# Longer runs of gathers and scatters on GpSimd, and eight message slots

## The chip, the cores and the metric
The kernel runs on one core of a Trainium2 chip. The metric is the device time of one execution in microseconds (us), as the median of several runs. TensorE (PE), VectorE (DVE), ScalarE (ACT), GpSimd (POOL) and SyncE (SP) are the core's engines. Each runs its own list of instructions, and they keep in step by semaphores.

## The reference
The kernel computes one layer of a graph network over 50000 nodes with 128 float32 features, and 50000 edges, sorted by receiver (`dst`):

```
w   = MLP(radial_embedding(edge_length))            # 8 -> 64 -> 64 -> 128, silu
ss, vv = (x_scalars @ W_up0)[senders], (x_vectors @ W_up1)[senders]
mid = products of w, ss, vv and the edge's direction  # 64 scalars, 64 vectors
msg = segment_sum(mid, receivers) @ W_out           # back to 128 features
x   = layernorm(x + msg / 16)
```

So each edge gathers the row of its sender from `x`, makes a message of 128 numbers, and adds it to the row of its receiver. Receivers are unevenly spread: many edges end at low node numbers. The second part normalises all 50000 rows.

## The kernel before
**Units.** The edges are dealt into 98 units of four tiles with 128 edges each, from the highest receivers down. The dealing is such that tiles which follow each other closely lie apart in the sorted order; neighbouring pieces of the order stand four tiles apart. A table `scatter_orders`, computed in the kernel, says for each unit how far the copy of `x` must have come and whether its tiles share rows.

**The accumulator.** SyncE copies `x` to the internal tensor `acc`, in 80 pieces of 312.5 KB from the high rows down (`acc_init`). Each unit's messages are added to `acc` by four indirect DMAs of 128 rows, `scatters` (line 470, `acc<-msg,index`). The rows of the senders come by four indirect DMAs, `gathers` (line 444, `sender<-in_x_dram,index`). All 784 are issued by GpSimd.

**The arithmetic of a unit.** TensorE transposes the gathered rows (`turn`, line 531), projects them, runs the two hidden layers and the weights, then sums equal receivers by a matmul with the equality matrix `same` and projects out. ScalarE moves results from PSUM and applies silu. VectorE forms products (`products`), the equality matrix and the count of earlier equal receivers (`equal_receivers`, line 923, one comparison per tile whose two inputs are in SBUF), and the rows to scatter to (`receiver_rows`). ScalarE writes the finished message of unit v to slot v % `RING` of the tile `msg` (`msg_out`, lines 672 and 673). From unit `RING` on it waits until the unit that had the slot has been scattered.

**The dense part.** As `acc` becomes final from the top, SyncE loads chunks of 1664 rows (`total<-acc`, 832 KB, line 343, 30 of them), VectorE takes the statistics (line 986 and following), ScalarE normalises (line 724) and SyncE stores. A table `dense_orders` gives each pair of units its chunk. SyncE waits in pair j for the landing of both units (`landed`) and loads the chunk that stands for pair j + 5; VectorE takes that chunk's first statistics in its pair j + 4, ScalarE normalises it in its pair j + 5. SyncE does all this in order.

**GpSimd's order, which the change touches.** GpSimd's program is written out for all units. It gathers units 0 to 5 first (`LAG` is 6). Then, for each pair of units v, v + 1: read the two entries of the table (line 450), gather units v + 6 and v + 7, scatter units v and v + 1. `sender` has eight slots, so that `gathers(u)` waits until unit u - 8 has been transposed (line 440), and each gather waits for the landing of the gather four tiles ago (line 443). A scatter waits for the needed pieces of `acc_init` (lines 454, 455), for its rows (457) and its message (458), for the landing of the scatter four tiles ago (line 463, three in the first two units), and, where the table says that rows are shared, of the one just before (line 468).

Of the kernel before, what the change touches and what calls it, by code (L numbers as in the profile page):

```python
# [24 lines left out]
P = 128  # L25
# [9 lines left out]
G = 4  # L35
ROWE = G * P
UNITS = -(-E // ROWE)
FULL = E // ROWE
TILES = UNITS * G
PAIRS = UNITS // 2  # L40
LAG = 6
RING = 4
SRING = 8
BATCH = 2
STATS_AFTER = 4
NORM_AFTER = STATS_AFTER + 1
RATE = 3 / 4
# [14 lines left out]
ROUNDS = 3  # L62
SSTEPS = 5 + 3 * ROUNDS
RSQRT_BITS = float(0x5f3759df)
assert UNITS % 2 == 0 and LAG <= SRING and UNITS % BATCH == 0 and (UNITS - 2) % G == 0 and (UNITS - 2) % SRING == 0 and UNITS <= P and FULL == UNITS - 1 and FULL >= 96
assert NORM_AFTER > STATS_AFTER and NORM_AFTER > RING // 2 and (UNITS - 2) % RING == 0 and CHUNKS % 2 == 0 and PIECES % 2 == 0 and N % PIECE == 0 and N - CHUNK - (CHUNKS - 1) * STEP in range(REST + 1)


def bass_gnn(nc, x, src, dst, edge_vec, edge_len, W_up0, W_up1, w0, b0, w1, b1, w2, b2, W_out0, W_out1, out):
# [5 lines left out]
    with ctx:  # L75
        def sb(name, shape, dt=F32):
            return ctx.enter_context(nc.sbuf_tensor(name, shape, dt))
# [85 lines left out]
        sumT = sb("sumT", [P, 2, G, 2, P])  # L163
        msg = sb("msg", [P, RING, G, D])

# [231 lines left out]
        def _(pool):  # L397
# [35 lines left out]
            def here(u, i):  # L433

                return (slot_done[u][i], 16) if u < 2 else (gathered[u % 2][i], 16 * (u // 2))

            def gathers(u):

                if u >= SRING:
                    pool.wait_ge(senderT_ps, u - SRING + 1)  # L440
                for i in range(G):
                    if u >= 1:
                        pool.wait_ge(*here(u - 1, i))
                    pool.indirect_dma_start(sender[:, u % SRING, i, :], None, x,  # L444
                                            bass.IndirectOffsetOnAxis(ap=index[:, u, 0, i:i + 1], axis=0)
                                            ).then_inc(here(u, i)[0], 16)

            def order_of(v):

                return pool.value_load(scatter_orders[0:1, v:v + 1], min_val=2, max_val=2 * PIECES - 1)  # L450

            def scatters(v, order):

                pool.wait_ge(acc_init[0], 16 * (order // 4) + 16)  # L454
                pool.wait_ge(acc_init[1], 16 * ((order + 2) // 4))  # L455
                meets = order % 2
                pool.wait_ge(rows_ready, v + 1)
                pool.wait_ge(msg_ready, v + 1)
                for i in range(G):
                    n = G * v + i  # L460
                    far = 3 if v < 2 else 4
                    if n >= far:
                        pool.wait_ge(*landed(n - far))
                    for of in range(n - far + 1, n) if i == 0 else (n - 1,):
                        if of >= 0:

                            to, count_after = landed(of)
                            pool.wait_ge(to, count_after - 16 + 16 * meets)  # L468
                    pool.sem_inc(pool_passed, 1)  # L469
                    pool.indirect_dma_start(acc, bass.IndirectOffsetOnAxis(ap=index[:, v, 1, i:i + 1], axis=0),  # L470
                                            msg[:, v % RING, i, :], None, compute_op=ALU.add
                                            ).then_inc(slot_done[v % 2][i], 16)
# [3 lines left out]
                gathers(u)  # L476
            pool.wait_ge(spare_rows, 16)
            pool.wait_ge(scatter_tables, 1)
            for v in range(0, UNITS, BATCH):
                orders = [order_of(u) for u in range(v, v + BATCH)]  # L480
                for u in range(v + LAG, min(v + LAG + BATCH, UNITS)):
                    gathers(u)
                for u in range(v, v + BATCH):
                    scatters(u, orders[u - v])


# [131 lines left out]
        def _(act):  # L618
# [46 lines left out]
            def msg_out(v, k):  # L665
                b = k % 2
                act.wait_ge(msg_ps, v + 1)
                slot = bass.ds(v % RING, 1)
                if k >= RING:
                    for i in range(G):  # L670
                        act.wait_ge(slot_done[b][i], 8 * (v - b) - 8 * RING + 32)
                act.copy(msg[:, slot, :, 0:MUL].rearrange("p s i k -> p (s i) k"), ps_msg[:, :, 0:MUL])  # L672
# [405 lines left out]
```

## Time and profile before

| | us |
|---|---|
| median of three runs | 1268.94 (1268.22 to 1271.01) |
| profiled execution | 1267.58 |
| its span, first to last instruction | 1265.8 |
| POOL busy | 1007.1 (80%) |
| PE busy | 860.4 (68%) |
| DVE busy | 695.9 (55%) |
| ACT busy | 535.5 (42%) |

The mean granted TensorE clock was 0.842 of full speed. Busy times count an engine's instructions only; the time that its sequencer needs to issue a DMA is idle time before it, named "issue". The releaser of an idle time is what the semaphores name as last. The HBM moved 123 GB/s over the span.

### The profile page before, as it was taken

To read this page: it belongs to the slowest core of one execution; us is meant where nothing else is said; L and a number is where in the kernel's file an instruction comes from. 1 tells how busy PE (TensorE), PEld (TensorE's weight loads), DVE (VectorE), ACT (ScalarE), POOL (GpSimd) and SP (SyncE) were. 2 spreads that over 40 slices of the span, in tenths; PEclk is the share of its full clock that TensorE was granted. 3 is DMA by queue.
4 is the path that set the end of the run, shared out by engine and by line. 5 is a ranking of instruction groups with operands and counts; after the bars stand their busy time and mean duration, and the time that the engine had idled before them with its cause. 6 is when DMAs were issued, how large, how long until landed. Compare 5 with 4: busy or idle time off the path is not lost.

```text
span 1265.8 us, 25804 instructions
## 1 busy us (share of the span) xinstructions
PE 860.4 (68%) x6206; PEld 817.6 (65%) x6206; DVE 695.9 (55%) x2905; ACT 535.5 (42%) x1416; POOL 1007.1 (80%) x818
## 2 busy tenths in 40 slices
PE   1899775776677667766776677667756775677550
PEld 1799665776577657765776577567756775677550
DVE  6766443575466556565476366446654656446422
ACT  5445322354355245434443435335524533444321
POOL 7778788878877887888778887887888788877885
PEclk9989888888888888888888888878887888788875
DMA  5788784444444443543444443444444354353434
GB/s 161 189 182 193 188 191 71 71 97 93 96 95 98 93 95 46 147 94 41 100 120 69 93 108 87 93 94 97 98 93 95 57 136 94 41 115 84 89 36 86
DMA packets 82645, 130.55 MB, mean 103 GB/s; under 512 B 16168, under 2 KB 66859, under 8 KB 81328
## 3 DMA queue, kind: packets, MB, share of 16 engines
q0 software_dynamic: 68992, 51.43, 31.1%
q1 hardware_dynamic: 12936, 77.36, 17.5%
q10 hardware_dynamic: 680, 1.38, 0.3%
q14 instruction: 28, 0.23, 0.1%
q8 instruction: 9, 0.15, 0.1%
HBM read 78.40 MB, written 77.31 MB: 123 GB/s over the span
## 4 chain that ended last, share of the span: by engine, by line
POOL 44%; issue 27%; DMA 19%; POOLq 4%; SPq 2%; PE 2%; DVE 1%; ACT 0%; DVEq 0%; ACTq 0%
POOL acc L470 30%; POOL sender L444 14%; DMA acc<-msg,index 8%; DMA acc<-in_x_dram 6%; DMA sender<-in_x_dram,index 5%; POOLq L450 2%; POOLq L468 1%; POOLq L469 1%; SPq L307 1%; POOLq L455 0%; PE ps_sum L572 0%; PE ps_wts L559 0%; PE ps_msg L584 0%; PE ps_hid L543 0%; POOLq L454 0%
## 5 line engine op out<-in xcount | busy, mean ns | idle before, releaser
L470 POOL DMA_INDIRECT acc<-msg,index x392 | 616.8, 1573 | 120.8 <-issue 107.5
L444 POOL DMA_INDIRECT sender<-in_x_dram,index x392 | 382.9, 977 | 124.7 <-issue 110.4
L543 PE MATMUL ps_hid<-hid,mlp 128*128 128x256 f32 x196 | 86.3, 532 | 328.3 <-ACT hid L687 328.3
L957 DVE TENSOR_TENSOR wts<-ps_wts,bias 128x512 f32<-128x512 f32 x98 | 67.7, 691 | 423.5 <-PE ps_wts L559 423.5
L543 PEld LDWEIGHTS ps_hid<-hid,mlp 128*128 128x128 f32 x196 | 38.8, 248 | 336.5 <-ACT hid L687 336.5
L572 PEld LDWEIGHTS ps_sum<-same,mid 128*128 128x128 f32 x1568 | 238.1, 224 | 11.5 <-DVE mid L972 0.8
L572 PE MATMUL ps_sum<-same,mid 128*128 128x128 f32 x1568 | 244.8, 308 | 0.7 <-DVE mid L972 0.7
L672 ACT COPY msg<-ps_msg 128x128 f32 (+1 forms) x98 | 26.0, 265 | 426.5 <-DMA acc<-msg,index 381.2
L584 PE MATMUL ps_msg<-outw,sumT 128*128 128x64 f32 x1568 | 185.9, 272 | 0.0
L584 PEld LDWEIGHTS ps_msg<-outw,sumT 128*128 128x128 f32 x1568 | 182.8, 192 | 0.0
L663 ACT COPY sumT<-ps_sum 128x512 f32<-128x512 f32 x196 | 114.6, 584 | 143.0 <-PE ps_sum L572 141.6
L724 ACT ACTIVATE normed<-total,shift,rstd 128x128 f32 x392 | 157.4, 482 | 34.9 <-DVE shift L1022 31.2
L559 PE MATMUL ps_wts<-mlp,hid 128*128 128x128 f32 x784 | 133.5, 327 | 0.6 <-ACT hid L699 0.6
L559 PEld LDWEIGHTS ps_wts<-mlp,hid 128*128 128x128 f32 x784 | 126.9, 245 | 1.3 <-ACT hid L699 1.3
L552 PE MATMUL ps_up<-up,senderT 128*128 128x128 f32 x784 | 115.3, 291 | 6.6 <-DVE mid L964 6.6
L552 PEld LDWEIGHTS ps_up<-up,senderT 128*128 128x128 f32 x784 | 96.5, 194 | 18.6 <-issue 7.0
L986 DVE BATCH_NORM_STATS2 stats<-total 128x6 f32 x392 | 78.8, 278 | 33.8 <-DMA total<-acc 32.9
L950 DVE TENSOR_TENSOR proj<-ps_up,vec_all 128x384 f32<-128x384 f32 x98 | 54.2, 553 | 74.3 <-issue 40.3
L923 DVE CUSTOM_DVE_ANT_0 junk<-same,earlier 128x128 f32<-128x128 f32 x392 | 91.4, 289 | 3.4
L538 PE MATMUL ps_hid<-basisT,mlp 32*128 32x128 f32 x392 | 69.8, 297 | 0.2 <-ACT basisT L679 0.2
L681 ACT COPY senderT<-ps_sT 128x512 f32<-128x512 f32 x98 | 56.5, 577 | 29.3 <-PE ps_sT L531 28.7
L673 ACT COPY msg<-ps_msg 128x384 f32 (+1 forms) x98 | 67.2, 685 | 0.1
(139 smaller groups left out, 1035.2 us busy)
## 6 DMA issues: line engine op xcount, KB each, us to landing
acc<-in_x_dram SPq DMA_DIRECT2D x80, 312.5 KB
total<-acc SPq DMA_DIRECT2D x30, 832.0 KB
out_dram<-normed SPq DMA_DIRECT2D x29, 832.0 KB, 4.2
sender<-in_x_dram,index POOLq DMA_INDIRECT x392, 2.6
acc<-msg,index POOLq DMA_INDIRECT x392, 3.3
out_dram<-normed ACTq DMA_DIRECT2D x1, 832.0 KB, 3.6
vec_raw<-in_edge_attr_dram SPq DMA_DIRECT2D x1, 576.0 KB
acc<-zeros SPq DMA_DIRECT2D x1, 320.0 KB, 4.1
```

Of the source, the lines that this page charges most:

```text
L444: pool.indirect_dma_start(sender[:, u % SRING, i, :], None, x, bass.IndirectOffsetOnAxis(ap=index[:, u, 0, i:i + 1], axis=0)).then_inc(her ...
L470: pool.indirect_dma_start(acc, bass.IndirectOffsetOnAxis(ap=index[:, v, 1, i:i + 1], axis=0), msg[:, v % RING, i, :], None, compute_op=ALU.add
L538: mm = pe.matmul(ps_hid[:, q, :], mlp0[:, q, :], basisT[:, b, :], start=True, stop=True)
L543: pe.matmul(ps_hid[:, 2:4, :], mlp1[:, :], hid0[:, k % 2, :], start=True, stop=True).then_inc(hid1_ps, 1)
L552: mm = pe.matmul(ps_up[:, i, :], senderT[:, b, P * i:P * (i + 1)], up[:, :], start=True, stop=True)
L559: mm = pe.matmul(ps_wts[:, i, :], hid1[:, b, P * (i // 2):P * (i // 2 + 1)], mlp2[:, i % 2, :], start=True, stop=True)
L572: mm = pe.matmul(ps_sum[r][:, i, h, :], mid[:, b, 2 * r + i, P * h:P * (h + 1)], same[:, b, 2 * r + i, :], start=True, stop=True)
L584: mm = pe.matmul(ps_msg[:, i, 2 * MUL * h:2 * MUL * (h + 1)], sumT[:, b, i, h, :], outw[:, h, :], start=True, stop=True)
L663: act.copy(sumT[:, b, 2 * r:2 * r + 2, :, :], ps_sum[r][:, :, :, :]).then_inc(sum_ready[r], 1)
L724: mm = act.activation(normed[:, b, r, :], total[:, quarter, r, :].rearrange("p b d -> p (b d)"), ACT.Identity, scale=rstd[:, b, r:r + 1], ...
L923: mm = dve.tensor_tensor_reduce(junk[:, b, i, :], same[:, b, i, :], earlier[:, :], 1.0, 0.0, ALU.mult, ALU.add, count[:, b, i:i + 1])
L986: mm = dve.bn_stats(stats[:, r, :], total[:, quarter, r, :].rearrange("p b d -> p (b d)"))
```

## The change
The ring of message slots grows from four to eight. GpSimd handles four units in a batch, not two: it reads four table entries, issues the gathers of four units (16 DMAs) and then the scatters of four units (16 DMAs). The first batch keeps two units, since (98 - 2) divides by four. The gathers still run to six units past the end of the batch. ScalarE's program follows the ring: its first `2 * (RING // 2 + 1)` units are written out, now 10 and not 6, and its loop over pairs starts at pair 5; the table has no chunk for the pairs before. Nothing else changes.

```
-RING = 4
+RING = 8
 SRING = 8
-BATCH = 2
+BATCH = 4
...
-            for v in range(0, UNITS, BATCH):
-                orders = [order_of(u) for u in range(v, v + BATCH)]
-                for u in range(v + LAG, min(v + LAG + BATCH, UNITS)):
-                    gathers(u)
-                for u in range(v, v + BATCH):
+            gathered_to = LAG
+            for v, w in [(0, 2)] + [(v, v + BATCH) for v in range(2, UNITS, BATCH)]:
+                orders = [order_of(u) for u in range(v, w)]
+                while gathered_to < min(w + LAG, UNITS):
+                    gathers(gathered_to)
+                    gathered_to += 1
+                for u in range(v, w):
                     scatters(u, orders[u - v])
```

## Rows read from the trace of the kernel before

**Rows 1.** Busy and costliest groups of the page: busy us, mean ns, idle before.
```profile
L470 POOL DMA_INDIRECT acc<-msg,index x392 | 616.8, 1573 | 120.8 <-issue 107.5
L444 POOL DMA_INDIRECT sender<-in_x_dram,index x392 | 382.9, 977 | 124.7 <-issue 110.4
```

**Rows 2.** Waits: engine, line, releaser, total us, times, longest us.
```profile
ACT msg L672 <- DMA acc<-msg,index: 381.2, 45, 10.3
...
DVE stats L986 <- DMA total<-acc: 32.9, 2, 25.8
...
POOL acc L470 <- DMA acc<-msg,index: 11.2, 34, 1.1
...
POOL sender L444 <- PE ps_sT L531: 0.3, 1, 0.3
POOL acc L470 <- DMA acc<-in_x_dram: 0.3, 1, 0.3
POOL acc L470 <- ACT msg L673: 0.3, 1, 0.3
```

**Rows 3.** Timeline of POOL, one round: start, duration, instruction, idle before.
```profile
603.61 1.02 POOL L444 DMA_INDIRECT sender<-in_x_dram,index  x1 [0.30 <-issue]
604.93 0.98 POOL L444 DMA_INDIRECT sender<-in_x_dram,index  x1 [0.30 <-issue]
606.21 0.94 POOL L444 DMA_INDIRECT sender<-in_x_dram,index  x1 [0.30 <-DMA sender<-in_x_dram,index]
607.46 0.94 POOL L444 DMA_INDIRECT sender<-in_x_dram,index  x1 [0.30 <-issue]
...
613.70 1.62 POOL L470 DMA_INDIRECT acc<-msg,index  x1 [0.30 <-issue]
615.63 1.58 POOL L470 DMA_INDIRECT acc<-msg,index  x1 [0.30 <-issue]
617.52 1.57 POOL L470 DMA_INDIRECT acc<-msg,index  x1 [0.30 <-DVE index L937]
619.39 1.55 POOL L470 DMA_INDIRECT acc<-msg,index  x1 [0.30 <-issue]
621.25 1.55 POOL L470 DMA_INDIRECT acc<-msg,index  x1 [0.30 <-issue]
...
628.68 1.02 POOL L444 DMA_INDIRECT sender<-in_x_dram,index  x1 [0.30 <-issue]
```

**Rows 4.** Timeline of POOL, the last run of 32 scatters, first two and last.
```profile
1193.98 1.62 POOL L470 DMA_INDIRECT acc<-msg,index  x1 [0.30 <-issue]
1195.91 1.59 POOL L470 DMA_INDIRECT acc<-msg,index  x1 [0.30 <-issue]
...
1251.86 1.57 POOL L470 DMA_INDIRECT acc<-msg,index  x1 [0.30 <-issue]
```

**Rows 5.** Windows: stretch and length, busy us and count by engine, clock, DMA share, GB/s.
```profile
83.24:1193.98 1110.74, 790.08 (x5729) 752.06 (x5727) 620.16 (x2622) 483.01 (x1283) 895.46 (x705) 0.85 0.48 99
1193.98:1253.41 59.43, 21.00 (x149) 19.89 (x149) 15.84 (x69) 10.46 (x23) 49.98 (x32) 0.69 0.46 65
```

**Rows 6.** Chain of waits around 599 us: POOL's sequencer reads two table entries.
```profile
598.51 0.16 POOLq L450
...
599.26 0.02 POOLq L450
```

**Rows 7.** Timeline of ScalarE: messages of units 2 and 3 written.
```profile
74.67 0.27 ACT L672 COPY msg<-ps_msg 128x128 f32<-128x128 f32 x1 [0.94 <-PE ps_msg L584]
...
82.23 0.27 ACT L672 COPY msg<-ps_msg 128x128 f32<-128x128 f32 x1 [0.94 <-PE ps_msg L584]
```

**Rows 8.** Line 470: landings from 580 us, from 60 to 380, from 1236; a load.
```profile
DMA to landing us min/median/max: 3.2/3.3/3.6
...
DMA to landing us min/median/max: 3.2/3.4/5.6
...
DMA to landing us min/median/max: 3.2/3.3/3.5
...
1240.89 0.36 SPq L343 DMA_DIRECT2D total<-acc  x1
```

**Rows 9.** Timelines of POOL and VectorE around the fourth gather of the next round.
```profile
632.53 1.04 POOL L444 DMA_INDIRECT sender<-in_x_dram,index  x1 [0.30 <-issue]
...
632.46 0.28 DVE L923 CUSTOM_DVE_ANT_0 junk<-same,earlier 128x128 f32<-128x128 f32 x1
```

More of the change, by code:

```diff
@@ L64 @@
 RSQRT_BITS = float(0x5f3759df)
-assert UNITS % 2 == 0 and LAG <= SRING and UNITS % BATCH == 0 and (UNITS - 2) % G == 0 and (UNITS - 2) % SRING == 0 and UNITS <= P and FULL == UNITS - 1 and FULL >= 96
+assert UNITS % 2 == 0 and LAG <= SRING and (UNITS - 2) % BATCH == 0 and (UNITS - 2) % G == 0 and (UNITS - 2) % SRING == 0 and UNITS <= P and FULL == UNITS - 1 and FULL >= 96
 assert NORM_AFTER > STATS_AFTER and NORM_AFTER > RING // 2 and (UNITS - 2) % RING == 0 and CHUNKS % 2 == 0 and PIECES % 2 == 0 and N % PIECE == 0 and N - CHUNK - (CHUNKS - 1) * STEP in range(REST + 1)
```

## The prediction
> **What bounds the kernel now.** I read the busy times first. GpSimd (POOL) is the busiest engine, and two instructions make up nearly all of its 1007.1 us: 392 scatters and 392 gathers, 1573 and 977 ns each [rows 1]. The idle times come next. Before a gather or scatter POOL idles 0.30 us, the same for both kinds, and the profile finds no releaser for most of it (107.5 and 110.4 us in all). A real wait is rare: 11.2 us over 34 scatters for an earlier scatter's landing, one gather for TensorE's transpose, one scatter for a message, 0.3 us each [rows 2]. In the other direction, ScalarE waited 381.2 us in 45 places, up to 10.3 us, to put a message into a slot that a scatter had not yet left. So the arithmetic waits for POOL, never POOL for the arithmetic. From 83.24 to 1193.98 us POOL runs 44 equal rounds of eight scatters and eight gathers, then 32 scatters in a row until 1253.41 us [rows 5]; some 12 us of finishing follow. Whatever shortens POOL's stream by one microsecond ends the kernel one earlier; whatever only speeds up the others gives nothing.
>
> **What a switch costs.** The timeline of POOL through one quiet round is the core of this case; the reader should subtract neighbouring starts [rows 3]. Gathers: 1.32, 1.28, then 1.25 us from start to start. Scatters: 1.93, 1.89, 1.87, then 1.86. The first two gathers after a scatter, and the first three scatters after a gather, are slower than those that follow. Over the settled steps that is (0.07 + 0.03) + (0.07 + 0.03 + 0.01) = 0.21 us a round. The gap stays at 0.30 and the instruction itself is longer (1.02 and 0.98 against 0.94; 1.62 and 1.58 against 1.55), so it is POOL's own work that is slow after a change of kind, not a wait. The last run bears this out: its first two scatters take 1.62 and 1.59 us, and the 32nd 1.57 [rows 4]; the surcharge does not come back with the count of instructions.
>
> **The change part by part.**
> *Longer runs.* Before, a run of gathers stands ahead of each pair of units from v = 2 to v = 90: 45 runs behind the opening 32 gathers. After, one stands ahead of v = 2, 6, ... 90: 23 runs (16 gathers each, the last 8). Scatter runs fall from 46 to 24. So 22 rounds of switching vanish: 22 x 0.21 = 4.6 us. The counts, 392 and 392, stay, and so do the settled steps. The opening and the last 32 scatters are the same in both: units 96 and 97 are gathered ahead of scatter 90 either way.
>
> *Reads of the order table.* Four register loads, not two, now stand ahead of a run of gathers on POOL's sequencer. Two take from 598.51 to about 599.28, 0.8 us [rows 6], while POOL has scatters queued: the gather behind them starts at 603.61 [rows 3]. Four take 1.6 us, and 3.5 us of cover remain: cost 0. Without the cover, 23 x 1.6 less what is hidden today, at most 37 us; with 5.1 us of queued work I take the nil end. A gain isn't possible, as the number of loads is the same.
>
> *Eight message slots.* ScalarE's wait now asks for the scatter of eight units ago. It can run further ahead, which POOL does not notice directly. What is late next: VectorE. Its statistics are paired with units, and a dense chunk is loaded only when the units of four pairs ago have landed; up to now four slots held the arithmetic back more than that, and VectorE waited for a load only twice [rows 2]. I expect that wait to appear in most pairs and to replace part of ScalarE's. Behind it on VectorE stand the next unit's products and rows, so messages stop too. But then six messages are ready, 6 x 4 x 1.86 = 44.6 us of scatters, more than a run of 16 (29.8 us), and the load is a matter of some 5 us. Cost 0.
>
> *Gathers further ahead.* Gather u asks that unit u - 8 has been transposed. For the last of a run that is unit v + 1, transposed before message v - 1 was made, which the preceding scatters already needed. Cost 0. In the first such run (gathers 8 to 11 from 73.0 us on, the scatters of 2 to 5 from about 93 us) messages 2 and 3 were written at 74.67 and 82.23 us already [rows 7], each later one some 7.6 us on, against 7.4 us for a unit's scatters with 18 us of lead.
>
> *Scatter after scatter.* A scatter waits for the landing of the one four before. In a run of eight half of them look back across the gathers; in a run of 16 only a quarter. The distance within a run is 4 x 1.86 = 7.44 us, less the 0.30 that an issue takes: landing may last some 7.1 us. It lasts 3.3 in the middle and at most 5.6 beside the copies of x [rows 8]. Cost 0; the bounds are in the rivals. The pieces of `acc` needed move earlier by less than a round, and POOL's waits for them were one scatter, 0.3 us.
>
> *Irregular lengthening.* The 44 rounds last 1110.74/44 = 25.24 us, the quiet one 628.68 - 603.61 = 25.07 [rows 3, 5]. So 0.17 us a round, 7.5 us in all, is in single instructions that are longer, such as the fourth gather of the next round, 1.04 instead of 0.94 us, while VectorE runs the comparison with two inputs from SBUF [rows 9]. The number of VectorE instructions is unchanged, but the phase between the two engines is not. I take no change; bounds: halved with the rounds, a gain of 22 x 0.17 = 3.7 us; doubled, a loss of 7.5 us.
> The Trainium skill (SBUF — State Buffer, the rules on the shared port pair) says that a VectorE instruction with two SBUF inputs contends with a GpSimd instruction that reads SBUF, and that the later one is blocked until the first ends. The row would allow that reading; the slip of 0.10 us is less than the 0.28 us of the comparison. By the rule a collision depends on phase alone, so it names the cause of the last bound above and not its sign.
>
> **The sum.** The profiled execution took 1267.58 us (span 1265.8 and 1.8 around it); less 4.6 that is 1263.0. The median of the runs is 1268.94, 1.36 higher, so on its scale the forecast is 1264.3.
>
> **The rivals.**
> *More than the switches goes (faster).* If the lengthenings belong to the rounds, since many sit at the same place (third or fourth gather), they halve too: 8.3 us gained, 1260.6. For it: their fixed place. Against: VectorE's work, beside which they occur, is not less.
> *The switch is not saved (no change).* If the slow first instructions come from something else, such as a period in time or in instructions, regrouping moves them only: 1268.9. Against it is the last run of 32, where nothing returns [rows 4].
> *Landings become the bound (slower).* Place: the landing wait inside a run of 16. A dense load of 832 KB goes out when an odd unit has landed. Today that is always the end of a run, so the load falls beside gathers; after the change half of the 30 loads go out in the middle of a run, beside the scatters of the other two units. Price: beside copies of 312.5 KB, landings rose from 3.3 to 5.6, that is 2.3 us; if it grows with size, 2.3 x 832/312.5 = 6.1 and a landing is 9.4 us, 2.3 over the 7.1 allowed. Fifteen loads at 2.3 us are 35 us: 1268.94 - 4.6 + 35 = 1299. It decides once a landing is above about 7.1 + 4.6/15 = 7.4 us. For it: the DMA engines are shared. Against it: in the last run one such load was issued at 1240.89 us amid scatters, and no landing there passed 3.5 us [rows 8].
> The Trainium skill (DMA: Bandwidth & Descriptors, section on queues, rings and completion order) has the rule that speaks against the change: each DMA engine serves its queue rows in turn, packet by packet, so a large load does delay a scatter's packets. By that rule alone the landings inside the run would lengthen; the trace agrees for the copies and shows next to nothing for the load.
> *Collisions double (slower, barely).* The lengthenings grow by 7.5 us in longer gather runs that lie wholly beside arithmetic: 1268.94 - 4.6 + 7.5 = 1271.8.
>
> **How the numbers follow.** Forecast 0.62; more saved 0.21; no change 0.07; landings 0.05; collisions 0.05. This kernel can tell about 0.2% (2.5 us) from no change. The forecast's own spread (the surcharge from durations instead of steps gives 0.24 a round, 5.3 us; a collision more or less) is some 2 us to either side, so 0.02 of it falls inside 0.2%. Faster: 0.62 + 0.21 - 0.02 = 0.81. Slower: the landings and 0.02 of the collisions, whose price lies just at the bound, 0.07. Same: the rest, 0.07 + 0.02 + 0.03 = 0.12. The range runs from the case with more saved, 1260.6, rounded down to 1260.3, to 1267.8, which leaves out the two slower cases and most of the one without change.
>
> **What would show it.** Right: POOL's timeline with 16 gathers and 16 scatters in a row, surcharges only at the first two or three of each; no idle beyond 0.30 us in a run; summed time of the gathers and scatters down by about 4.6 us from 999.7; VectorE's waits for `total` up from two to a few dozen, ScalarE's wait for slots down; last scatter near 1247. Wrong: POOL idle for an earlier scatter's landing beyond 0.30 us in the second half of a run (landings), gathers longer than 0.94 in the middle of a run in greater number (collisions), a surcharge that comes back at the ninth instruction (no switch), or any POOL wait for a message.

## The result and the profile after

The changed kernel is slower: 1275.17 us (median of six runs, 1271.6 to 1276.88) against 1268.72 for the kernel before (six runs), a ratio of 1.0046 with a 95% interval of 1.003 to 1.0062. The forecast was 1264.3. The profiled execution took 1275.54 us, its span 1273.6. A ratio, here and below, compares undisturbed executions alone and need not be the quotient of the medians.

The groups of the page that answer to [rows 1], with two that rose (busy us, mean ns, idle before):

```profile
L470 POOL DMA_INDIRECT acc<-msg,index x392 | 617.9, 1576 | 121.6 <-issue 103.7
L444 POOL DMA_INDIRECT sender<-in_x_dram,index x392 | 377.8, 964 | 135.6 <-issue 123.2
L533 PE MATMUL ps_sT<-ident,sender 128*128 128x128 f32 x392 | 85.6, 318 | 305.5 <-DMA sender<-in_x_dram,index 305.5
...
L988 DVE BATCH_NORM_STATS2 stats<-total 128x6 f32 x392 | 78.8, 278 | 125.7 <-DMA total<-acc 125.4
```

The gathers are busy 5.1 us less (the saved switches are 2.2 of it, the rest is fewer lengthened gathers); the scatters, which should have saved the other 2.4 us, are busy 1.1 us more. POOL idles 10.9 us more before gathers (124.7 to 135.6). The page calls most of that "issue", so the groups alone don't say what it waits for. The waits of the others moved as foretold, if less far: ScalarE's wait for a slot fell from 381.2 us [rows 2] to 10.2, VectorE's for dense loads rose from 2 to 21 times (of 49 pairs, so not most of them), and TensorE now stands 305 us for gathered rows:

```profile
DVE stats L988 <- DMA total<-acc: 125.4, 21, 34.2
...
ACT msg L674 <- DMA acc<-msg,index: 10.2, 13, 1.3
```

Where POOL loses is seen in its timeline. This is a run of 16 gathers, later in the program than the round of [rows 3] (units 68 to 71), with SyncE's issues below (start, duration, instruction, idle before):

```profile
835.92 1.02 POOL L444 DMA_INDIRECT sender<-in_x_dram,index  x1 [0.30 <-issue]
837.24 0.98 POOL L444 DMA_INDIRECT sender<-in_x_dram,index  x1 [0.30 <-issue]
838.53 0.94 POOL L444 DMA_INDIRECT sender<-in_x_dram,index  x1 [0.30 <-issue]
...
841.03 0.95 POOL L444 DMA_INDIRECT sender<-in_x_dram,index  x1 [0.30 <-issue]
...
844.78 0.94 POOL L444 DMA_INDIRECT sender<-in_x_dram,index  x1 [0.30 <-issue]
847.29 0.94 POOL L444 DMA_INDIRECT sender<-in_x_dram,index  x1 [1.57 <-issue]
848.53 0.94 POOL L444 DMA_INDIRECT sender<-in_x_dram,index  x1 [0.30 <-issue]
...
838.01 0.36 SPq L343 DMA_DIRECT2D total<-acc  x1
840.73 0.36 SPq L358 DMA_DIRECT2D out_dram<-normed  x1
```

The ninth gather idles 1.57 us in place of 0.30. It looks back at the fifth (841.03), and that one went out 0.3 us after a dense store and 3.0 after a dense load. The chain of waits shows it step by step (start, duration, what held POOL up):

```profile
841.03 4.70 DMA sender<-in_x_dram,index
845.73 0.02 issue
845.75 0.02 POOLq L443
845.77 1.52 issue
847.29 0.94 POOL sender L444
```

The fifth gather lands 4.70 us after its start. Line 443 is the landing wait, passed by POOL's sequencer at once; the ninth gather starts 1.52 us later. This second part matters: 4.70 us alone is less than the 5.0 us between the fifth gather and the ninth. The ninth is the first gather of its unit, and the trace shows its landing wait as an instruction of its own on the sequencer. For a gather inside a unit there is none, and the lag is short: in this run the third gather landed at 843.28 and the seventh started at 843.54.

Later than 220 us, nine runs have this stall, 0.9 to 1.4 us each beyond the settled step, 10.0 us together, and they are exactly the nine in which a load and a store were issued 2 and 5 us behind the first gather. By the trace's semaphore records the fifth gather landed in 4.3 to 4.7 us in these nine and in at most 2.6 in the other late runs; the lag behind line 443 was 1.52 us in eight of them and 1.85 in one. (Of the three runs before 220 us one has a shorter idle at the ninth gather, 0.78 us with a lag of 0.72, another at the tenth, 0.57. What sets the lag stays open.) In the late runs between there is none; this is the eighth to the tenth gather of the next run, without a load:

```profile
896.27 0.94 POOL L444 DMA_INDIRECT sender<-in_x_dram,index  x1 [0.30 <-issue]
897.52 0.94 POOL L444 DMA_INDIRECT sender<-in_x_dram,index  x1 [0.30 <-issue]
898.77 0.95 POOL L444 DMA_INDIRECT sender<-in_x_dram,index  x1 [0.30 <-issue]
```

The account of the whole, from POOL's timeline: each step from start to start, less the settled step at its place in the run (1.32, 1.28, 1.25 for gathers, 1.93, 1.89, 1.87, 1.86 for scatters), summed; "early" is up to 220 us, while `x` is copied.

| us beyond the settled steps | gathers early | gathers later | scatters early | scatters later | last scatter starts |
|---|---|---|---|---|---|
| before | 0.7 | 4.2 | 1.7 | 1.6 | 1251.86 |
| changed | 1.3 | 10.5 | 3.8 | 4.9 | 1259.53 |

So the loss is 0.6 + 6.3 + 2.1 + 3.3 = 12.3, and less the 4.6 of the switches 7.7, which is how much later the last scatter starts (1259.53 - 1251.86 = 7.67). The finish behind it takes 14 us in both.

### The profile page after: what moved, and what is told of

Read it like the earlier page. It is cut to its first block, busy times and chain, and to the rows that moved or that the text cites. A ratio compares the mean times of both kernels' runs of the same rounds, so it can differ in the third digit from the quotient of the medians.

```text
span 1273.6 us, 25748 instructions
## 1 busy us (share of the span) xinstructions
PE 872.5 (69%) x6206; PEld 816.7 (64%) x6206; DVE 692.7 (54%) x2905; ACT 534.6 (42%) x1416; POOL 1003.1 (79%) x818
## 4 chain that ended last, share of the span: by engine, by line
POOL 38%; DMA 30%; issue 24%; POOLq 5%; SPq 2%; PE 1%; DVE 1%; DVEq 0%; ACT 0%
POOL acc L470 23%; DMA acc<-msg,index 16%; POOL sender L444 14%; DMA acc<-in_x_dram 10%; DMA sender<-in_x_dram,index 4%; POOLq L450 3%; POOLq L468 1%; SPq L307 1%; POOLq L469 0%; PE ps_msg L586 0%; PE ps_sum L574 0%; POOLq L455 0%; PE ps_up L554 0%; POOLq L463 0%; SPq L329 0%
## 5 line engine op out<-in xcount | busy, mean ns | idle before, releaser
L444 POOL DMA_INDIRECT sender<-in_x_dram,index x392 | 377.8, 964 | 135.6 <-issue 123.2
L533 PE MATMUL ps_sT<-ident,sender 128*128 128x128 f32 x392 | 85.6, 318 | 305.5 <-DMA sender<-in_x_dram,index 305.5
L533 PEld LDWEIGHTS ps_sT<-ident,sender 128*128 128x128 f32 x392 | 52.1, 152 | 327.5 <-DMA sender<-in_x_dram,index 327.3
L574 PE MATMUL ps_sum<-same,mid 128*128 128x128 f32 x1568 | 228.7, 294 | 0.7 <-DVE mid L974 0.7
L586 PE MATMUL ps_msg<-outw,sumT 128*128 128x64 f32 x1568 | 219.9, 302 | 0.0
L586 PEld LDWEIGHTS ps_msg<-outw,sumT 128*128 128x128 f32 x1568 | 217.7, 222 | 0.0
L554 PE MATMUL ps_up<-up,senderT 128*128 128x128 f32 x784 | 134.3, 323 | 9.7 <-DVE mid L966 9.7
L554 PEld LDWEIGHTS ps_up<-up,senderT 128*128 128x128 f32 x784 | 113.5, 223 | 24.2 <-issue 16.4
L561 PE MATMUL ps_wts<-mlp,hid 128*128 128x128 f32 x784 | 104.6, 277 | 0.6 <-ACT hid L701 0.6
L561 PEld LDWEIGHTS ps_wts<-mlp,hid 128*128 128x128 f32 x784 | 96.2, 193 | 1.3 <-ACT hid L701 1.3
L540 PEld LDWEIGHTS ps_hid<-basisT,mlp 32*128 32x128 f32 x392 | 59.9, 216 | 17.1 <-ACT basisT L681 10.0
```

What stands on the lines that cost most here:

```text
L533: mm = pe.transpose(ps_sT[:, P * i:P * (i + 1)], sender[:, k % SRING, i, :], ident[:, :])
L540: mm = pe.matmul(ps_hid[:, q, :], mlp0[:, q, :], basisT[:, b, :], start=True, stop=True)
L554: mm = pe.matmul(ps_up[:, i, :], senderT[:, b, P * i:P * (i + 1)], up[:, :], start=True, stop=True)
L561: mm = pe.matmul(ps_wts[:, i, :], hid1[:, b, P * (i // 2):P * (i // 2 + 1)], mlp2[:, i % 2, :], start=True, stop=True)
L574: mm = pe.matmul(ps_sum[r][:, i, h, :], mid[:, b, 2 * r + i, P * h:P * (h + 1)], same[:, b, 2 * r + i, :], start=True, stop=True)
L586: mm = pe.matmul(ps_msg[:, i, 2 * MUL * h:2 * MUL * (h + 1)], sumT[:, b, i, h, :], outw[:, h, :], start=True, stop=True)
```

## The experiments

The runs fell on several chips, each group beside the kernel before on its own. On most it takes 1268 to 1269 us, on one 1448. Theory A says that the ninth gather waits for a landing delayed by the dense transfers; theory B, that scatter landings or collisions with VectorE make the loss. The ninth gather, as the first of its unit, also waits for a transpose (line 440); the edit of the look back leaves that wait as it is, and so tells the two apart.

### On a chip where the kernel before takes 1448 us

**The changed kernel again.**


> The changed kernel as it is, for a second trace and times beside the kernels below. Theory A (gather landings): in every round in which a dense load and a dense store are issued some 2 and 5 us after the first of the 16 gathers, the ninth gather idles 1.2 to 1.7 us instead of 0.30, because it waits for the landing of the fifth, which shares the DMA engines with both; nine such rounds, about 10 us in all, and none in the other rounds. Theory B (scatter landings and collisions): the longer steps lie among the scatters and move about from one execution to the next. Both: 1275 us; B expects the stalls of the ninth gather to be absent or elsewhere.

**Gathers look back eight tiles.** The previous DMA on the same semaphore is the one eight tiles ago, so that a count still names one DMA.
```
-                    if u >= 1:
-                        pool.wait_ge(*here(u - 1, i))
+                    if u >= 2:
+                        pool.wait_ge(*here(u - 2, i))
```


> The changed kernel, but each gather waits for the landing of the gather eight tiles ago, not four. Theory A: the ninth gather then waits for the first, long landed, the fifth is watched only by the thirteenth, 10 us later; the stalls of 0.9 to 1.4 us in nine or ten rounds go, 10 us in all: 1275 - 10 = 1265, which would be 4 us under the kernel before, about the 4.6 us of the saved switches. Theory B: the waits of gathers are not the cause, 1275 less at most 2. A third case, that the DMA engines' work itself is the limit: the wait moves to the scatters behind, 1273 or more.

**The same edit in the kernel before.**


> The kernel before with the same edit alone: each gather waits for the landing of eight tiles ago. Theory A: a run of eight gathers looks back only at its first four, which land before the dense load has begun, so nothing is to be won: 1268.7, within 1 us. If 3 us or more go here too, the gather's wait cost something already before and E1's gain is not special to the long runs.

**Eight slots alone** (`RING = 8` in the kernel before).


> The kernel before with eight message slots and nothing else. Theory A: the ring changes when the arithmetic runs, not POOL's runs: 1268.7 within 1.5 us, while ScalarE's wait for a slot (381 us before) turns into VectorE's wait for dense loads and TensorE's for gathered rows. Theory B in the form of collisions: the new phase between VectorE and POOL lengthens single gathers and scatters, 1271 to 1274.

Measured: changed 1396.87 us, ratio 0.9718 (0.9624 to 0.9812); with the longer look back 1400.01, 0.975 (0.9681 to 0.9818); the edit in the kernel before 1443.12, 1.0076 (1.0026 to 1.0125); eight slots alone 1445.53, 1.0026 (0.9968 to 1.0084). The kernel before spreads over 1418 to 1470 us here, so that these ratios are rougher than the others. The two edits of the kernel before changed little, but the changed kernel *gains* 2.8% here, and the longer look back adds nothing to it. The expectations were written for the other sort of chip, and the kernel is bound otherwise on this one. Timelines of POOL, ScalarE and TensorE in the changed kernel's trace:

```profile
671.81 1.57 POOL L470 DMA_INDIRECT acc<-msg,index  x1 [0.30 <-issue]
676.90 1.55 POOL L470 DMA_INDIRECT acc<-msg,index  x1 [3.53 <-DVE index L939]
...
674.90 0.27 ACT L674 COPY msg<-ps_msg 128x128 f32 x1 [8.96 <-remote]
...
670.09 0.37 PE L574 MATMUL ps_sum<-same,mid 128*128 128x128 f32 x1 [1.37 <-issue]
672.22 0.37 PE L574 MATMUL ps_sum<-same,mid 128*128 128x128 f32 x1 [1.75 <-issue]
672.95 0.56 PE L574 MATMUL ps_sum<-same,mid 128*128 128x128 f32 x1 [0.36 <-issue]
674.37 0.56 PE L574 MATMUL ps_sum<-same,mid 128*128 128x128 f32 x1 [0.86 <-issue]
```

The scatter at 676.90 is the first of the 44th unit: 172 scatters were issued ahead of it, four for each of 43 units, and 43 messages had been written. Its message was written at 674.90. So here POOL does wait for messages; the releaser named (VectorE's index) is wrong. TensorE is what is late: it stands 0.4 to 1.8 us between matmuls of one group, which the program puts behind each other with no wait between, and 9.7 us ahead of a group for "issue" in this stretch. What holds its instructions up on that chip stays open, and so does why longer runs suffer less from it. For the question at hand the four runs say nothing, so I repeated three of them elsewhere.

### On chips where it takes 1268 to 1269 us

**Runs of one unit**, `BATCH = 1`, `RING = 4`.


> The kernel before with runs of one unit: four gathers, then four scatters, four slots. 50 gather runs and scatter runs more than before. If a switch costs 0.21 us, this is 1268.7 + 10 = 1279 on a chip where the kernel before takes 1268.7, with the longer first steps standing at every fourth instruction. If the switch costs nothing and only the place of the long steps moves: 1269. Where landings are slow enough that the first of a run's later scatters waits for the landing of its first (seen on a chip where the kernel before took 1448), shorter runs look back across the gathers and that wait goes, which would make this kernel faster there than the kernel before.

Measured 1281.18, ratio 1.0099 (1.0082 to 1.0116), 12.7 us more. The switches are 46 more, not the 50 that I wrote, 9.7 us; in the profiled execution the steps beyond the settled ones grew by 4.3 (later scatters rose from 1.6 to 10.6, later gathers fell from 4.2 to 0.8; why, stays open). POOL's timeline shows both surcharges at every fourth instruction:

```profile
111.45 1.02 POOL L444 DMA_INDIRECT sender<-in_x_dram,index  x1 [0.30 <-issue]
112.77 0.98 POOL L444 DMA_INDIRECT sender<-in_x_dram,index  x1 [0.30 <-issue]
114.06 0.94 POOL L444 DMA_INDIRECT sender<-in_x_dram,index  x1 [0.31 <-issue]
...
116.56 1.62 POOL L470 DMA_INDIRECT acc<-msg,index  x1 [0.30 <-issue]
118.48 1.58 POOL L470 DMA_INDIRECT acc<-msg,index  x1 [0.30 <-issue]
120.37 1.56 POOL L470 DMA_INDIRECT acc<-msg,index  x1 [0.30 <-issue]
```

The price of a switch holds.

**The changed order with four slots**, `RING = 4`.


> The changed order of GpSimd with the four message slots of before. Theory A (the wait of the ninth gather for the fifth's landing, beside a dense load and store): the stalls depend on the order alone, so they stay, but with four slots the scatters of a run must be fed while they run, one message per 7.44 us against 7.55 us that the arithmetic needs for a unit and more with dense work in it: POOL then waits for messages in the second half of each run, some us in each of 22 rounds, 1290 or more. If eight slots do not matter: as the changed kernel, 1275.

Measured 1274.05, 1.0048 (1.0031 to 1.0064), as the changed kernel. The stalls of the ninth gather are there, and I was wrong that the scatters would starve: ScalarE waits 415.0 us for slots, POOL not for messages. Neither the saved switches nor the stalls need the slots.

**Gathers look back eight tiles, again** (the edit above).


> The changed kernel with each gather waiting for the landing of the gather eight tiles ago, not four, again, to meet a chip on which the kernel before takes 1268 to 1269. Theory A: the stalls of the ninth gather beside a dense load and a dense store go, some 10 us: 1265. Theory B: gathers' waits are not the cause, 1273 to 1275.

**The changed kernel beside it.**


> The changed kernel as it is, beside the one above, on the same chip. 1275, with the ninth gather idle for 1.2 us and more in nine or so of the 22 rounds and only there where a dense load was issued some 2 us behind the first gather.

Measured on one chip: 1261.51, 0.9948 (0.9934 to 0.9962), against 1274.26, 1.0044 (1.0028 to 1.0059). One wait moved is worth 12.7 us and makes a kernel that beats both. The trace of the first, in the same part as above:

```profile
825.19 1.02 POOL L444 DMA_INDIRECT sender<-in_x_dram,index  x1 [0.30 <-issue]
...
834.04 0.95 POOL L444 DMA_INDIRECT sender<-in_x_dram,index  x1 [0.30 <-issue]
835.29 0.95 POOL L444 DMA_INDIRECT sender<-in_x_dram,index  x1 [0.30 <-DMA sender<-in_x_dram,index]
...
827.25 0.35 SPq L343 DMA_DIRECT2D total<-acc  x1
829.97 0.36 SPq L358 DMA_DIRECT2D out_dram<-normed  x1
```

The load and the store go out at the same distance, 2.1 and 4.8 us behind the first gather, and the ninth gather (835.29) starts on time. Beside it the unchanged wait shows the nine stalls again, 9.6 us. The two profiled executions lie 16.3 us apart, further than the medians. Later gathers make 9.8 of it (10.2 us beyond the settled steps with the old wait, 0.4 without), early gathers 3.0 (3.2 and 0.2), early scatters 1.8 (3.6 and 1.8), later scatters 0.9 (4.9 and 4.0). The fifth gather still lands late in the nine runs, after 4.2 to 4.8 us; it merely holds nobody up.

**Small dense stores.**
```
-  out[... CHUNK rows ...]  <-  normed[:, b, :, :]
+  out[... P rows ...]      <-  normed[:, b, 0:1, :]
```


> The changed kernel, where SyncE's dense stores write one row of 13 from each partition (64 KB, not 832 KB, so that most of the output is left out), with the same places and waits. Theory A: the load alone keeps the DMA engines busy until some 4 to 5 us after its issue; the fifth gather, 5.0 us after the first and 2.9 after the load's issue, is then delayed less, and most of the stall at the ninth goes: 1267 or less. If the load alone does it: the stalls stay, 1274.

Measured 1264.59, 0.9965 (0.9952 to 0.9978). All nine stalls are gone though the wait is as in the changed kernel and each load is still there. The DMA share tells why: 12 us from the first gather in 40 slices of 0.3 us, digits in tenths, for the kernel before (830.4 on), the changed one (second trace, 836.6 on) and this one (828.9 on):

```profile
DMA  3991043005928989998999998979630700070000
```
```profile
DMA  2990035000934589899999999999744600070000
```
```profile
DMA  0991035000995479999987470034000700061007
```

With load and store the engines are full from some 4 us behind the first gather to some 8.5; with the load alone they are full to about 6.3 and nearly idle from 7.2. The fifth gather, issued at 5.1, falls into the middle; with small stores it lands in 2.6 to 3.0 us. The first row is the lesson of the case: the kernel before had the same full engines at the same place, and so the same late gathers. In its 18 rounds with load and store later than 220 us the records of the fifth gather's landing end 4.1 to 4.7 us after its start (some lack a few entries, so that they may be low), in the others at most 2.9 us after it. Its run of eight ended before any instruction looked back at the fifth.

**Runs of eight units**, `BATCH = 8`, with the longer look back.


> Runs of eight units (32 gathers, 32 scatters), with gathers waiting for eight tiles ago. By the price of a switch, 0.21 us, 12 switch pairs fewer than in the changed kernel: 2.5 us under the first kernel of this group, 1262 to 1263. If the arithmetic can't feed 32 scatters in a row from what six gathered units and eight slots hold, POOL waits for messages: 1275 and more.

Measured 1270.31, 1.001 (1.0 to 1.0019): the saving of 2.5 us is more than lost, though POOL waits for no message to speak of. The steps beyond the settled ones are 12.7 us more than in the kernel of four units with the same look back. Part is the reads of the table, whose cover is gone. The eight reads ahead of the gather below occupy POOL's sequencer from 171.51 to 176.10, and the last scatter ends at 175.32. The first gather of a run idles 0.3 to 1.6 us, once 3.41.

```profile
173.77 1.55 POOL L470 DMA_INDIRECT acc<-msg,index  x1 [0.30 <-issue]
176.94 1.02 POOL L444 DMA_INDIRECT sender<-in_x_dram,index  x1 [1.62 <-issue]
```

These gaps cost some 8 us together. The rest lies in single longer instructions.

**The kernel before with the longer look back.**


> The kernel before with gathers waiting for the landing of eight tiles ago, on a chip where it takes 1268 to 1269. In a run of eight gathers the last four look back at the first four, which landed before the dense load went out: nothing to win, 1268.3 within 0.8. If it gains 2 us or more, part of the 12.7 us that the same edit gave in the changed kernel is no matter of long runs.

Measured 1266.41, 0.998 (0.9971 to 0.9989), 2.7 us under the kernel before: more than I expected, and by the bound stated above a part that is no matter of long runs. In its trace early scatters are 0.1 beyond the settled steps, not 1.7, and later gathers 3.2, not 4.2; one trace each does not prove the places. The trace of the kernel before does show that gather landings cost it something already: a seventh or eighth gather idles 0.39, 0.53 and 0.61 us at three places later than 220 us, and the gather it looks back at landed only 4.9 to 5.1 us after its start, beside a dense load. With the longer look back no gather later than 220 us idles more than 0.31 us.

**Four units, longer look back, four slots.**


> Runs of four units, gathers waiting for eight tiles ago, but four message slots. The kernel with four slots and the old wait took as long as the changed one (1274.05 against 1274.3), so the slots are worth nothing there: 1261.5 expected here too, if the collisions between VectorE and POOL are as rare as with eight slots. With eight slots TensorE stood waiting for rows while POOL gathered; with four the arithmetic runs beside the gathers as before, and single gathers lengthen by some 4 us in all: then 1265.

Measured 1263.49, 0.9958 (0.9944 to 0.9972). The interval overlaps that of eight slots (0.9934 to 0.9962), and the two ran on different chips, so I can't tell them apart by time. By the trace both expectations are half right: later gathers are 3.6 us beyond the settled steps, against 0.4 with eight slots.

## Why the prediction was wrong

**The bound: right**, on all chips but one. POOL's stream set the end in every kernel on the chips of the prediction's kind.

**The price and the number of the switches: right.** 0.21 us a round, 22 rounds, 4.6 us. The steps after a switch are the same to 0.01 us in the changed kernel, and runs of one unit cost 12.7 us for 46 more switches, 9.7 of them by this price.

**Reads of the table: right** for four (later than 220 us the gap before the first gather stays 0.30); eight show where the cover ends.

**Eight slots: right** in what becomes late and in cost (with four, 1274.05 us); they were also not needed.

**The step that failed is the part "Gathers further ahead".** I checked the transpose that a gather waits for and priced the step at 0, and left out its other wait, for the landing of the gather four tiles ago, though it stands in the same function. I did such a sum for scatters alone. For gathers the distance is 4 x 1.25 = 5.0 us, and a gather beside the dense load and store lands in 4.3 to 4.7 us. Set against the distance less an issue, as I did it for scatters, that would still have come out at next to nothing: the sum also needs the 1.52 us from the sequencer's wait to the start of a unit's first gather, which leaves such a gather 5.0 - 1.52, about 3.5 us, for the landing. 4.70 + 1.52 - 5.0 is 1.2 us, and the stall shown is 1.57 - 0.30 = 1.27. A run of eight has one such gather inside it, the fifth, and that looks back at the first, which lands in 2.6 us, ahead of the load's traffic. In a run of 16 the ninth looks back at the fifth, in the middle of load and store. (Some expectations say that the first four gathers have landed before the load goes out. They have not: the load goes out 2.0 to 2.3 us behind the first gather, and in the kernel before the third, issued half a microsecond behind it, lands in 4.3 to 5.0 us. The gather that looks back at it, the seventh, is inside a unit and mostly just in time.) The nine stalls together cost ten us.

**The rival "landings" had the mechanism and the wrong place.** It named the landing wait inside a run of 16, shared DMA engines and the dense loads, and set all of it among the scatters, where the new loads would fall. There it is nearly nil on this sort of chip (all waits of scatters for scatters rose from 11.2 to 15.1 us), though 20 of the 30 loads now went out amid scatters (2 before), not the 15 that I had counted. The loads that were always beside gathers did the harm, since the gathers were now watched there. With the chances as given, it had 0.05.

**"Irregular lengthening", taken as unchanged: wrong in the split.** Single scatters later than 220 us lengthen by 3.3 us more than before. The rows that show how: a first scatter of a run that starts while VectorE multiplies two SBUF operands (line 970) takes 1.87 us, not 1.62.

```profile
958.58 1.87 POOL L470 DMA_INDIRECT acc<-msg,index  x1 [0.30 <-issue]
...
958.41 0.55 DVE L970 TENSOR_TENSOR mid<-mid,vec_all 128x384 f32<-128x384 f32 x1
```

The same pair stands at the tenth scatter of another run, 874.11 with 1.86 us beside line 970 from 873.99 on. In the changed kernel 16 scatters later than 220 us take more than 1.7 us, and all 16 start while VectorE runs an instruction with two SBUF inputs, line 970 or the comparison of line 925; in the kernel before there are 6, all beside that multiplication. The rule of the Trainium skill quoted ahead (SBUF — State Buffer, the rules on the shared port pair) names such a meeting. The same section infers, on the other side, that such an instruction does not hold up the writing of descriptors. The size does not follow from the rule either: the first scatter above is 0.25 us longer, while 0.38 us of the multiplication were left. No run here took the VectorE instruction away, so the cause is argued and not shown. In return the gathers are almost free of it once nothing stalls: 0.4 us with eight slots and the longer look back, against 4.2 before. I read this as TensorE waiting for rows while POOL gathers, so that VectorE rests too; with four slots it was 3.6, which agrees. All steps beyond the settled ones are then 6.4 us, against 8.2 before, and with the 4.6 of the switches that accounts for nearly all of the 6.6 us that this kernel gained.

**The rule on shared queues** (Trainium skill, DMA: Bandwidth & Descriptors, section on queues, rings and completion order) pointed the right way: large transfers do delay a gather's packets, and the trace agrees, with landings of 4.3 to 4.7 us for the fifth gather beside a dense load and store, against a median of 2.6 for gathers.

## What to carry to other kernels

When a run of like instructions is lengthened, list every wait in the issuing function and ask for each at which place of the run it now looks back, and what else is under way there. A late transfer costs nothing until somebody watches it; the full DMA engines were visible in the old profile, and only the watcher was new. And a completion wait should look back as far as its semaphore permits, here eight tiles and not four. Where a wait stands as an instruction of its own on the sequencer, add the time from there to the start of the work, here 1.52 us, to what the wait must be ahead by.

## What the runs showed of the hardware that was not expected

On one chip the kernel before takes 1448 us in place of 1268: TensorE stands up to 1.8 us between matmuls that wait for nothing, POOL then waits for messages, and the same change that costs 0.5% on the others gains 2.8%. POOL starts a gather 1.52 us after its sequencer has passed a landing wait that stands apart (eight of the nine late stalls, 1.85 us in the other), but 0.26 us after the landing in a case where none stands apart; both times are hidden as long as the landing is early. GpSimd's first indirect DMA after one of the other kind takes 0.07 to 0.08 us longer and the second 0.03 to 0.04, whatever the length of the runs (4, 8, 16 or 32).
